# Adding the attention mask on TensorE: a bf16 identity matmul into the score bank in place of additions on GpSimd

## What is computed

```
q = (x @ Wq + bq).reshape(B, S, 16, 32).transpose(0, 2, 1, 3)      # k, v alike
scores = einsum('bhqd,bhkd->bhqk', q / sqrt(32), k) + attention_bias   # (16, 16, 512, 512)
scores = where(src_mask, -inf, scores)                                 # mask (16, 1, 512, 512)
probs = softmax(scores)
ctx = einsum('bhqk,bhkd->bhqd', probs, v)
x = x + (ctx @ Wo + bo)
h = layernorm(x) * g2 + beta2
ff = gelu2(h @ W1 + b1) @ W2 + b2
out = x + ff
```

## Time and profile before

| | us |
|---|---|
| median of 3 runs (5175.97 to 5199.07) | 5191.7 |
| the profiled execution | 5190.59 |
| its span, first to last instruction | 5188.7 |
| TensorE busy | 4193.0 (81%) |
| VectorE busy | 3240.6 (62%) |
| GpSimd busy | 2447.1 (47%) |
| ScalarE busy | 2391.5 (46%) |
| GpSimd's mask additions (L634), 520 of them | 1139.4 |
| TensorE's score blocks (L913), 1024 of them | 505.6 |
| mean granted clock of TensorE | 0.915 |

### The profile page before, as it was taken

One profiled execution on the slowest core, in us unless ns is written; L12 is line 12 of the kernel. 1 busy time (PEld: TensorE's weight loads), 2 busy tenths in 40 slices (PEclk: granted clock), 3 DMA queues, 4 the chain that ended last, 5 costly groups with the idle time before them and its releaser, 6 DMA issues.

```text
span 5188.7 us, 80793 instructions
## 1 busy us (share of the span) xinstructions
PE 4193.0 (81%) x24872; PEld 3051.9 (59%) x24872; DVE 3240.6 (62%) x6332; ACT 2391.5 (46%) x4459; POOL 2447.1 (47%) x1164
## 2 busy tenths in 40 slices
PE   7985787888888787877878787878878787878788
PEld 3431565666666565656656565656656565656566
DVE  8972556565655656565665657575756656565656
ACT  0002544546364545545363645545363635445363
POOL 0000554545555554545555554545555554545455
PEclk9995899999999899999989899999999899999989
DMA  3223744535353634535363635535363636445362
GB/s 119 108 91 77 208 134 130 163 104 178 101 171 116 181 127 138 162 105 171 95 187 100 184 124 156 152 111 165 99 185 102 178 122 168 141 123 171 95 177 84
DMA packets 541110, 713.65 MB, mean 138 GB/s; under 512 B 45600, under 2 KB 257872, under 8 KB 540592
## 3 DMA queue, kind: packets, MB, share of 16 engines
q1 hardware_dynamic: 523728, 674.35, 44.2%
q10 hardware_dynamic: 16896, 33.56, 1.7%
HBM read 537.42 MB, written 35.72 MB: 110 GB/s over the span
## 4 chain that ended last, share of the span: by engine, by line
PE 32%; issue 18%; DVE 17%; SPq 10%; POOL 6%; ACT 3%; DMA 3%; DVEq 0%; ACTq 0%; POOLq 0%
PE bank L844 20%; SPq L534 10%; PE bank L889 4%; POOL prob L634 4%; PE bank L913 2%; DVE xin L1077 2%; PE bank L925 2%; DMA stack<-parts 2%; DVE prob L1115 2%; PE bank L853 1%; DVE wide L1203 1%; DMA prob<-in_fside_Bx16xSxS 1%; PE bank L948 1%; ACT gel L810 1%; ACT parts L814 1%
## 5 line engine op out<-in xcount | busy, mean ns | idle before, releaser
L634 POOL TENSOR_TENSOR prob<-prob,mask_add 128x1024 f32<-128x1024 f32 x520 | 1139.4, 2214 | 323.1 <-DMA prob<-in_fside_Bx16xSxS 322.6
L623 POOL TENSOR_TENSOR w<-w_raw,w 128x1024 fp32r<-128x1024 f32 x243 | 607.4, 2500 | 995.0 <-ACT w L693 993.5
L925 PE MATMUL bank<-ident,prob 128*128 128x128 f32 x4096 | 679.0, 292 | 122.3 <-ACT probT L720 102.6
L702 ACT ACTIVATE prob<-prob,low 128x512 f32<-128x512 f32 x1024 | 731.8, 716 | 99.0 <-DVE low L1115 96.5
L913 PE MATMUL bank<-stack 128*128 128x512 f32 x1024 | 505.6, 496 | 323.3 <-DVE low L1115 169.5
L1115 DVE CUSTOM_DVE_ANT_0 prob<-bank,prob 128x512 f32<-128x512 f32 x1024 | 699.4, 684 | 0.0
L925 PEld LDWEIGHTS bank<-ident,prob 128*128 128x128 f32 x4096 | 516.1, 149 | 291.7 <-ACT probT L720 82.3
L623 POOL TENSOR_TENSOR stack<-V,stack 128x1024 fp32r<-128x1024 f32 x145 | 348.5, 2405 | 639.0 <-ACT stack L693 638.6
L720 ACT ACTIVATE probT<-bank 128x512 f32<-128x512 f32 x768 | 451.5, 590 | 355.8 <-PE bank L925 354.6
L1114 DVE COPY fence<-cur 128x1 f32<-128x1 f32 x1024 | 154.0, 150 | 622.9 <-PE bank L913 597.0
L844 PE MATMUL bank<-xT,stack 128*128 128x512 f32 x1944 | 493.2, 404 | 46.8 <-DVE xT L1086 34.3
(11 more groups left out here) (180 smaller groups left out, 6599.7 us busy)
## 6 DMA issues: line engine op xcount, KB each, us to landing
prob<-in_fside_Bx16xSxS SPq DMA_DIRECT2D x520, 512.0 KB, 4.5
stack<-parts SPq DMA_DIRECT2D x1024, 128.0 KB, 2.4
V<-in_L_cond_W SPq DMA_DIRECT2D x256, 256.0 KB, 4.2
w_raw<-in_L_cond_W SPq DMA_DIRECT2D x256, 256.0 KB, 3.1
xin<-x SPq DMA_DIRECT2D x17, 1024.0 KB, 5.6
w_raw<-in_L_cond_Wv SPq DMA_DIRECT2D x68, 256.0 KB, 2.8
field<-in_x SPq DMA_DIRECT2D x16, 1024.0 KB, 5.3
x<-total ACTq DMA_DIRECT2D x16, 1024.0 KB, 5.8
```

Source lines behind the costliest of these rows:

```text
L623: pool.tensor_tensor(w[s][:, 1, :], w_raw[s], w[s][:, 0, :].bitcast(F32), ALU.subtract).then_inc(w_lo[s], 1)
L634: pool.tensor_tensor(half, half, mask_add[:, q:q + 1, :].to_broadcast([P, 2, S]), ALU.add).then_inc(bias_masked, 1)
L702: act.activation(prob[:, i, :], prob[:, i, :], ACT.Exp, bias=low[:, i:i + 1], scale=-1.0, accum_out=total[:, g % 2, i:i + 1]).then_inc(exp ...
L925: mm = t.transpose(turned[e % 2][:, k * P:(k + 1) * P], prob[:, i, k * P:(k + 1) * P], ident[:])
```

## The change

Three things are changed together.

1. TensorE adds the mask. Behind each score matmul, which now leaves its accumulation open, stands a second one into the same bank: a 128 x 128 identity in bf16 (`mask_eye`) times the 128 x 512 mask rows of the query tile. TensorE waits once a batch for `mask_ready`, and once at the start for `mask_eye`.
2. GpSimd no longer adds masks: `add_mask` and its calls are gone, 520 operations in all, and one cast of the identity to bf16 is new.
3. VectorE's bias addition waits for the load of the bias (`bias_in`) instead of the masked bias; the conversion of the mask no longer waits for GpSimd.

```diff
+        mask_eye = sb("mask_eye", [P, P], BF16)
...
-                def add_mask(b, g, q, halves=(0, 1)):
-                    for h in halves:
-                        pool.wait_ge(bias_in[q][h], 16 * (4 * b + g + 1))
-                        half = prob[:, HG * q + 2 * h:HG * q + 2 * h + 2, :]
-                        pool.tensor_tensor(half, half, mask_add[:, q:q + 1, :].to_broadcast([P, 2, S]), ALU.add).then_inc(bias_masked, 1)
-
                 def group(b, g):
 
                     split_lo(0, ITEMS[0] * b + W0_QK + g + 2)
-                    for q in range(TB):
-                        add_mask(b, g + 1, q)
-
+
+                pool.wait_ge(keep["ident_in"], 16)
+                pool.tensor_copy(mask_eye[:], ident[:]).then_inc(eye_ready, 1)
                 for q in range(TB):
                     root(q + 1, q)
...
-                pool.wait_ge(mask_ready, 1 + START)
-                for q in range(TB):
-                    add_mask(0, 0, q)
                 pool.wait_ge(consts_in, 16 * 12)
...
-                    pool.wait_ge(mask_ready, b + 2 + START)
                     for f in range(8, NF):
                         split_lo(*chunk_item(b, f // 4, f % 4))
-                        add_mask(b + 1, 0, (f - 8) // 2, (f % 2,))
...
-                    t.matmul(score[i % 2][:], stack[g % 2][:, j, 0, q * P:(q + 1) * P], stack[g % 2][:, j, 1, :], start=True, stop=True) \
-                        .then_inc(score_full, 1)
+                    t.matmul(score[i % 2][:], stack[g % 2][:, j, 0, q * P:(q + 1) * P], stack[g % 2][:, j, 1, :], start=True, stop=False)
+                    t.matmul(score[i % 2][:], mask_eye[:], mask_add[:, q, :], start=False, stop=True).then_inc(score_full, 1)
...
+                t.wait_ge(eye_ready, 1)
                 for k in range(KB):
                     input_turn(0, k)
                 input_products(0)
                 with t.Fori(0, B) as b:
+                    t.wait_ge(mask_ready, b + 1 + START)
...
                     v.wait_ge(mask_in, 16 * (b + 1))
-                    v.wait_ge(bias_masked, 32 * b + START)
...
                     if i % 2 == 0:
-                        v.wait_ge(bias_masked, 32 * b + 8 * g + i // 2 + 1 + START)
+                        v.wait_ge(bias_in[i // HG][i % HG // 2], 16 * (4 * b + g + 1))
```

More of the change, by code:

```diff
@@ L477, in layers @@
         qk_hi, qk_lo = sem("qk_hi"), sem("qk_lo")
-        bias_masked, score_full, scored, exped, inv_ready, inverted = (
-            sem(n) for n in ("bias_masked", "score_full", "scored", "exped", "inv_ready", "inverted"))
+        eye_ready, score_full, scored, exped, inv_ready, inverted = (
+            sem(n) for n in ("eye_ready", "score_full", "scored", "exped", "inv_ready", "inverted"))
         probT_full, pv_done, ctx_scaled = (sem(n) for n in ("probT_full", "pv_done", "ctx_scaled"))
@@ L504, in _ @@
                 for signal in (*w_hi, *w_lo, *proj_full, *proj_read, probT_full, tok_ready, mask_ready, mixed, ff2_done,
-                               pv_done, g_lo, turn_lo, scored, *turned_copied, ctx_scaled, bias_masked, out_ready):
+                               pv_done, g_lo, turn_lo, scored, *turned_copied, ctx_scaled, out_ready):
                     sp.sem_inc(signal, START)
```

## The result

The changed kernel takes **5152.6 us** (median of 6 runs, 5143.3 to 5157.9). The kernel before, on the same chip, takes 5180.2 us (6 runs, 5171.9 to 5199.1). The ratio is 0.9938, with a 95% interval of 0.9917 to 0.9959: faster by 0.6%, or 28 us. The prediction was 5203 us, no change, with a range of 5163 to 5250.

A forecast was written before the change was run, and what follows sets the result against it. The prediction took TensorE to bound the feed-forward, and a chain of copies, TensorE and VectorE each attention group. Terms 1 to 4 summed as +118 - 90 - 9 - 8 = +11 us, giving about 5203 us, range 5163 to 5250.

The forecast's parts named there:

- Term 4: Last group of the attention: added matmuls may keep TensorE's clock up; a fifth of 2.5 us a batch booked, 8 us gain.
- Term 1: Attention: 1024 added mask matmuls on TensorE at 0.235 us, partly hidden, lose 7.4 us a batch, 118 us in all.
- Term 2: Feed-forward: TensorE's stalls for VectorE's low part vanish once GpSimd's mask additions go; 5.6 us a batch, 90 us gain.
- Term 3: Batch 0: VectorE no longer waits for GpSimd's first mask, and its low parts are not slowed; 9 us gain.
- the clock holds in the whole attention: Rival, attention: the full clock gives 2.5 us a batch instead of 0.5, total 5171 us; chance 0.14.
- The 0.34 us matmul: Rival, attention: each added matmul costs 0.34 us, the loss becomes 171 us, total 5256 us; chance 0.14.
- the 0.13 us matmul: Rival, attention: each added matmul costs far less than its columns, 0.13 us, total 5151 us; chance 0.01.
- the stalls that stay: Rival, feed-forward: splits still hold up two operations of each normalisation, the stall gain halves, total 5248 us; chance 0.11.

The follow-up runs named there:

- kernel 1: The changed kernel without its mask matmuls, the mask not applied at all: 5089.7 us, ratio 0.9826 to the kernel before.
- kernel 2: The kernel before with the mask matmul added behind all 1024 score blocks, GpSimd still adding its masks: 5247.4 us, ratio 1.0119.
- kernel 3: The kernel before with the mask matmul added behind 29 of 64 blocks a batch, counted as hidden; GpSimd keeps all masks: 5171.5 us, ratio 0.9975.
- kernel 5: The changed kernel with the mask matmul issued twice behind every score block: 5288.5 us, ratio 1.0192 to the kernel before.
- kernel 9: The kernel before, no added matmul, with the last four masks of group 0 on GpSimd held back until the normalisations are over: 5100.9 us, ratio 0.9829.
- late masks: The kernel before, no added matmul, with GpSimd's last four masks of group 0 moved behind the last chunk's split: 5144.0 us, ratio 0.9919.
- kernel 8: The kernel before with the late masks and the hidden matmuls of kernel 3 together: 5140.5 us, ratio 0.9906.
- kernel 11: The changed kernel with mask matmuls in groups 0 to 2 alone, the last group's masks left out of the computation: 5155.3 us, ratio 0.9942 to before.
- kernel 6: The kernel before with the masks of group 0 alone as matmuls, GpSimd keeping groups 1 to 3: 5149.2 us, ratio 0.9922.
- kernel 4: The kernel before with the eight feed-forward mask additions on GpSimd moved, two into each odd chunk, no added matmul: 5185.5 us, ratio 0.9999.

## Why the prediction was wrong

The difference of the two profiled executions was to be +11 us and is -38.6. By the steps:

- **Term 4, the clock, is the step that failed.** It saw the low clock in the last group, put all of it at 2.5 us a batch, and booked a fifth, with no row for the fifth. Measured: the low clock in the attention fell from 18.8 to 4.0 us a batch. Blocks that run at the full clock in both kernels give the matmuls' own price (next point), 100 us. The attention took 58.8 us more, of which -4.6 belong to batch 0. That leaves 100 - 63.4 = 36 us or 2.3 us a batch for the clock, against 8 us booked: 28 us of the 50. The cause rests on kernels 1, 2, 3 and 5: the clock follows the matmuls and not GpSimd, matmuls off the path shorten the run, and a second dose costs its full price. The size is a remainder and not measured by itself: 9 of the 36 us lie in blocks 0 to 9, and against kernel 1, whose attention is 71.9 us shorter than the changed kernel's, the remainder is 28 us. It is also small beside the low time that went, 14.8 us a batch. That fits stretches in which TensorE waits for others as well (busy 5.58 of 7 us in the earlier trace rows), but no run shows the reason.
- **Term 1: the price was right, the count slightly high.** The pitch is 0.22 to 0.24 us, as taken from the earlier trace rows. Between bias additions at full clock in both, the two group changes went from 10.15 to 11.53 us (+1.38 each; 1.65 forecast) and blocks 51 to 63 from 14.3 to 15.9 (+1.6; 2.2 forecast for the last group). Blocks 0 to 9, which spend their first 4 us at the low clock in both, went from 10.8 to 12.7 (+1.9, as forecast). Together 6.3 us a batch or 100 us, at the lower bound of 100 to 133: 18 us of the miss. Blocks 45 to 51 never ran at full clock before the change, and count as nothing here. Of the seven blocks of a group change these intervals hold six; the seventh would show ahead of them, in blocks 13 to 19, whose sum did not grow (-0.3 us).
- **Term 2 was right**: 92.2 us (90 forecast; the recorded 12 and 4 batches at 6.2 and 4.6 us make 5.8 a batch, not 5.6, and so 92), 28.1 us of waits (under 30). Held operations fell from eight to four a batch; three in one normalisation, as the text has it, was chunk 11 alone. The gaps are one chunk behind the normalisations, not at them. Kernel 9 confirms the reason.
- **Term 3 was right**: 5.8 + 4.6 = 10.4 us (9 forecast). VectorE's first bias addition is at 543.57, and its low parts in batch 0 take 0.69 and 0.68 us, where the earlier trace rows had 3.80 and 2.17.
- **The level of before.** I started from 5191.7 us, the median of three runs. Six runs gave 5180.2, and nineteen in a later set 5183.5. That is 11.5 us of the absolute miss. From 5180.2 the same steps would have given 5191.5 with a lower end of 5151.5, so that the time lies under the range rests on this level as much as on the steps. The profiled execution of before was one of the slower ones, so its span overstates the change as well: 38.6 us by the spans, 27.6 by the medians. The 50 us split up above go by the spans.

The rival "the clock holds in the whole attention" had the right mechanism and, with 2.5 us a batch, nearly the right size; it had a chance of 0.14. That its total, 21 us less than before, is close to the measured 28 is in part luck: it keeps the 118 us of term 1, and measures against the level of before that was too high. What spoke against it in my text was that "the waiting for copies stays as long". It did stay (1.30 us before, 1.06 us after at such a place), and the clock rose nevertheless. The 0.34 us matmul, the 0.13 us matmul and the stalls that stay did not come.

The Trainium skill, "TensorE: Matmul & The Clock Gate", section "HAM oscillation — how this bites in real kernels", describes matmul streams that are cut by waits for DMA and swing between the two clocks, and advises to put more of the matmuls in a row before each wait. The earlier trace rows was such a place (0.51 at the end of the copies), and the runs agree in kind: with more matmuls in such stretches the low time there fell from 11.1 to 3.8 us a batch. A reader who holds term 4 against that page has a reason to give the rival more than 0.14.

## What to carry to other kernels

Where a granted clock below 1 stands in a stretch to which the change adds matmuls, price both ends (clock as before, clock full) and give them like chances; a fifth of the gain with no row for it is a guess. Work on TensorE in time where it waits anyway can pay for itself; a trial with such matmuls alone (kernel 3) tests it, though its gain of 12 us took ten executions to see. Where two engines hold each other up, count the operations that stand side by side before choosing another engine: a wait of 7 us put on the idle engine on purpose (kernel 9) gave more than moving all its masks to TensorE did.

## What the runs showed of the hardware

- Hidden matmuls can shorten a kernel. 29 added matmuls of 128x512 in bf16 a batch, 464 in all, took the time at the low clock in the three stretches of the attention from 18.8 to 7.2 us a batch and the run from 5183.5 to 5171.5 us. Beside the late masks the same matmuls gave 3.5 us, which is within the noise (kernel 8).
- The clock of a stretch depends on more than the stretch. The last group's low time fell from 12.2 us a batch (kernel 1) to 5.8 by matmuls in the groups ahead of it (kernel 11), while the 16 of group 0 alone, at the start of a batch (kernel 6), lifted nothing in the attention.
- Even a VectorE operation with one tensor input is held up by GpSimd: the first operation of a normalisation takes 0.54 us alone (the changed kernel) and 2.37 us when a mask addition on GpSimd began 0.5 us ahead of it (kernel 4). Where GpSimd began 0.4 us behind it, it took 0.54 us as well.
